# One pool of seven PSUM banks for scores and everything else, with banks and a new order written in the step table

## The reference

```python
qkv = x @ W_qkv                       # 16 heads of 16
q, k = _rope(q, k)
att = einsum('bhtd,bhsd->bhts', q, k) / sqrt(DH) + causal_mask
y = einsum('bhts,bhsd->bhtd', softmax(att), v) @ W_o
x = _layernorm(x + y)
gate = softmax(x @ Wg + bg)           # 8 experts, the 2 largest kept, renormalised
out = einsum('bseo,bse->bso', einsum('bsi,eoi->bseo', x, We) + be, gate_sparse)
x = _layernorm(x + out)
```

## Time and profile before

| | |
|---|---|
| median of 3 runs | 3101.23 us (3095.9 to 3102.56) |
| the profiled execution | 3113.54 us, its span 3111.8 us |
| busy share of the span | PE 95%, DVE 85%, ACT 58%, POOL 34% |
| mean granted clock of TensorE | 0.962 |
| chain that ended last | PE 79%, DVE 13%, issue 4%, DMA 1%, ACT 1% |

### The profile page before, as it was taken

The page is one execution under the profiler, slowest core; times in us unless marked ns, Lnnn a source line. Parts: engine busy times, 40 slices in busy tenths (PEclk is TensorE's granted clock), DMA queues, the critical chain, the costliest instruction groups (busy, mean ns, idle before and its releaser), DMA issues.

```text
span 3111.8 us, 58478 instructions
## 1 busy us (share of the span) xinstructions
PE 2962.5 (95%) x18752; PEld 1400.9 (45%) x18752; DVE 2656.9 (85%) x8449; ACT 1812.8 (58%) x4125; POOL 1053.1 (34%) x1295
## 2 busy tenths in 40 slices
...
DMA packets 136930, 143.84 MB, mean 46 GB/s; under 512 B 29080, under 2 KB 111280, under 8 KB 136368
## 3 DMA queue, kind: packets, MB, share of 16 engines
...
...
## 4 chain that ended last, share of the span: by engine, by line
PE 79%; DVE 13%; issue 4%; DMA 1%; ACT 1%; POOL 0%; SPq 0%; DVEq 0%; ACTq 0%; POOLq 0%
PE bank L1068 26%; PE attend L1164 16%; PE bank L1125 10%; PE scores L1142 9%; PE bank L1105 6%; PE bank L1114 4%; DVE maxima L919 3%; PE bank L1188 3%; DVE bank L916 3%; PE bank L1172 2%; PE bank L1093 1%; DMA x_in<-in_x 1%; PE bank L1179 1%; PE bank L1196 1%; PE bank L1228 1%
## 5 line engine op out<-in xcount | busy, mean ns | idle before, releaser
L787 ACT ACTIVATE weights<-scores 128x512 f32<-128x512 f32 (+3 forms) x3072 | 1330.8, 492 | 836.2 <-PE scores L1142 828.5
L916 DVE CUSTOM_DVE_ANT_0 bank<-bank,far_q 128x128 f32<-128x128 f32 (+3 forms) x2048 | 956.2, 516 | 147.3 <-PE bank L1125 136.2
L919 DVE TENSOR_REDUCE maxima<-bank 128x1 f32<-128x512 f32 x1024 | 646.7, 682 | 50.1 <-PE bank L1125 47.7
L1164 PE MATMUL attend<-weights,values 128*32 128x512 f32 (+3 forms) x6144 | 655.4, 513 | 0.0
L1125 PE MATMUL bank<-k_stack,q_stack 48*128 48x512 f16 (+3 forms) x3072 | 581.2, 340 | 44.3 <-DVE maxima_hi L916 16.8
L706 POOL TENSOR_SCALAR_AFFINE_SELECT weights<-weights 128x512 f32<-128x512 f32 x512 | 320.8, 636 | 883.8 <-ACT weights L787 883.8
L1142 PE MATMUL scores<-q_stack,k_stack 51*128 51x512 f16 (+3 forms) x3072 | 564.2, 337 | 20.9 <-ACT weights L787 10.7
L1125 PEld LDWEIGHTS bank<-k_stack,q_stack 48*128 48x128 f16 x3072 | 174.4, 95 | 478.3 <-issue 315.3
L1142 PEld LDWEIGHTS scores<-q_stack,k_stack 51*128 51x128 f16 x3072 | 169.8, 94 | 448.9 <-ACT weights L787 256.5
L1068 PE MATMUL bank<-wexp_hi,zT_hi 128*128 128x512 f32 x1024 | 366.7, 439 | 2.2
L695 POOL TENSOR_TENSOR rope<-rope,cos_sb 128x512 f32<-128x512 f32 x124 | 158.5, 1278 | 519.3 <-DVE rope_swap L963 519.3
...
## 6 DMA issues: line engine op xcount, KB each, us to landing
parts_scratch<-parts SPq DMA_DIRECT2D x128, 256.0 KB, 2.1
q_stack<-parts_scratch SPq DMA_DIRECT2D x384, 64.0 KB, 2.3
k_stack<-parts_scratch SPq DMA_DIRECT2D x384, 64.0 KB, 2.3
x_in<-in_x SPq DMA_DIRECT2D x64, 256.0 KB, 3.7
...
q_stack<-lowrows SPq DMA_DIRECT2D x384, 4.0 KB, 1.7
...
```

The lines of the kernel that those rows point to most:

```text
L787: act.activation(weights[:, n % NW, hh, c0:CH], st[(QUAD * n + hh) % NS][:, c0:CH], ACT.Exp, scale=DH ** -0.5).then_inc(S["weights_ready"], 1)
L916: dve.tensor_tensor_reduce(out=b[:, 0:w], in0=b[:, 0:w], in1=far_q[:, CH - w:CH], scale=1.0, scalar=-SENTINEL, op0=ALU.add, op1=ALU.max, a ...
L919: dve.tensor_reduce(dst, b[:, 0:w], AX.X, ALU.max).then_inc(fr, 1)
L1164: last = pe.matmul(pv[32 * j:32 * j + 32, c0:CH], values[:, (s + 1) % SLOTS, o:o + 32], weights[:, n % NW, j, c0:CH], start=kb == 0, stop= ...
```

## The change

Three banks for scores and four for the rest become one list `bk` of seven. ST steps get a bank like all others. In `pre`, `early` and `first` the places are as before (score steps in turn over banks 4 to 6, others over 0 to 3). For `mid` and `last` the tables are new: the order of steps differs, and behind each step with a bank stands its bank ("B.1.11.3/3" is step B.1.11.3 in bank 3). `room()` now looks up the last user of the bank in table order, whoever it was: if it was an ST, TensorE waits for that exp, else for the reader's count. The set of steps is the same.

```diff
-NB = 4
+NB = 7
@@ steps(): the word is cut at "/"
+def placed(table):
+    words = (word.partition("/") for word in table.split())
+    return dict(zip(steps(table), (int(b) if b else None for _, _, b in words)))
@@ two rows of the middle table, old and new
-ST.25.0 ST.25.1 B.2.4.0 B.2.4.1 MOE.0.2.3 B.1.8.2 B.1.8.3 YE.1.1 ST.25.2 ST.25.3 PV.24 B.1.9.0 B.1.9.1
-ST.27.0 ST.27.1 MOE.0.3.1 B.1.10.2 B.1.10.3 ST.27.2 ST.27.3 PV.25 PV.26 MASK.27 LOAD.2
+ST.24.0/4 ST.24.1/6 MOE.0.3.1/4 MASK.22 MOE.0.3.2/1 MOE.0.3.3/5 ZT.1.1/0 ZT.1.0/6 YT.1.0/1 ST.24.2/6 ST.24.3/2
+  PV.22 MASK.24 PV.23
+ST.25.0/4 ST.25.1/5 B.1.11.0/0 B.1.11.1/5 B.2.4.0/4 B.2.4.1/2 B.1.11.2/6 B.1.11.3/3 ST.25.2/3 ST.25.3/2 YE.1.1
+  LOAD.2 GL.1/1 QK.1.2/5 GLT.1/0 MASK.25
+ST.27.0/0 ST.27.1/4 B.2.4.2/0 B.2.4.3/5 B.2.5.0/1 B.2.5.1/2 B.2.5.2/3 B.2.5.3/4 ST.27.2/2 ST.27.3/3 PV.26
+  MASK.27
@@ banks()
-        for n, step in enumerate(s for s in plan(seg) if s[0] in BANKED):
-            out[seg, step] = n % NB
+        rest = 0
+        for step in plan(seg):
+            if seg in PLACED and step[0] in ("ST", *BANKED):
+                out[seg, step] = PLACED[seg][step]
+            elif step[0] == "ST":
+                out[seg, step] = NB - NS + (QUAD * step[1] + step[2]) % NS
+            elif step[0] in BANKED:
+                out[seg, step] = rest % (NB - NS)
+                rest += 1
@@ ledger()
+            if step[0] in ("ST", *BANKED):
+                add(f"users{bank(seg, step)}", seg, step)
+def user_before(c, step):
+
+    users = f"users{bank(c.seg, step)}"
+    here = BOOK[users, c.seg]
+    n = here.index(step)
+    while n == 0:
+        if c.seg == "pre":
+            return None, None
+        c = earlier(c)
+        here = BOOK.get((users, c.seg), [])
+        n = len(here)
+    return c, here[n - 1]
@@ TensorE
                 def room():
-                    if c.seg != "pre" or BOOK[f"bank{nb}", "pre"].index(step) > 0:
-                        pe.wait_ge(free[nb], c.below(f"bank{nb}", step, 1))
+                    then, user = user_before(c, step)
+                    if user and user[0] == "ST":
+                        pe.wait_ge(S["weights_ready"], then.at("weights_ready", user))
+                    elif user:
+                        pe.wait_ge(free[nb], then.at(f"bank{nb}", user))
@@ ST
-                    if c.seg not in START or QUAD * n + hh >= NS:
-                        pe.wait_ge(S["weights_ready"], c.below("weights_ready", step, NS))
-                    pe.matmul(st[(QUAD * n + hh) % NS][:, c0:CH], pair(k_stack, MROWS, s, hh, slice(kb * P, (kb + 1) * P)),
+                    room()
+                    pe.matmul(b[:, c0:CH], pair(k_stack, MROWS, s, hh, slice(kb * P, (kb + 1) * P)),
```

More of the change, by code:

```diff
@@ L166 @@
 """)
[L168 to L196, removed]
@@ L203 @@
[L203 to L222, removed]
@@ L232 @@
[L232 to L237, removed]
@@ L277 @@
-ST.47.0 ST.47.1 ST.47.2 ST.47.3 MASK.47 PV.45
-""")
+MIDDLE_TABLE = """
+XL.1
+ST.0.0/4 ST.0.1/0 XL.0 B.0.0.0/2 B.0.0.1/3 PV.46 B.0.0.2/1 B.0.0.3/0 ST.0.2/3 ST.0.3/1 B.0.1.0/4 B.0.1.1/6 MC.3
+  LOAD.0 PV.47 YE.3.1 B.0.1.2/1 B.0.1.3/5 B.0.2.0/2 B.0.2.1/3
+ST.1.0/1 ST.1.1/3 B.0.2.2/4 B.0.2.3/0 XT.0/6 YT.3.1/1 ST.1.2/0 ST.1.3/4 MASK.0 XT.1/5 XL.2 B.0.3.0/3 B.0.3.1/2
+  XL.3
+ST.2.0/4 ST.2.1/3 PV.0 MASK.1 ST.2.2/3 ST.2.3/2 MT.3/6 QK.0.0/1 MASK.2 B.0.3.2/2 B.0.3.3/3
+ST.3.0/0 ST.3.1/1 PV.1 ST.3.2/6 ST.3.3/1 MASK.3 B.0.4.0/6 B.0.4.1/0 ROPE.0.0 B.0.4.2/1 B.0.4.3/2 B.0.5.0/4
+  B.0.5.1/5
@@ new lines @@
+ST.4.0/6 ST.4.1/4 XT.2/3 XR.0 XT.3/6 QK.0.1/0 HT.0.0/6 HT.0.1/1 B.0.5.2/4 B.0.5.3/0 ST.4.2/6 ST.4.3/0 PV.2
+  B.1.0.0/5 B.1.0.1/1 B.1.0.2/4 B.1.0.3/3
+ST.5.0/1 ST.5.1/6 XR.1 ROPE.0.1 B.0.6.0/6 B.0.6.1/2 PV.3 CAST.0.0 YE.0.0 B.1.1.0/1 B.1.1.1/5 ST.5.2/6 ST.5.3/2
+  WO.0.0/0 B.1.1.2/4 B.1.1.3/6
+ST.6.0/0 ST.6.1/3 CAST.0.1 PV.4 ST.6.2/2 ST.6.3/0 B.0.6.2/3 B.0.6.3/1 WO.0.1/2 B.1.2.0/3 B.1.2.1/0
+ST.7.0/0 ST.7.1/2 B.0.7.0/6 B.0.7.1/5 R1.0 HT.1.1/4 QK.0.2/2 B.1.2.2/3 B.1.2.3/4 ST.7.2/6 ST.7.3/1 ROPE.0.2 PV.5
@@ new lines @@
+ST.8.0/5 ST.8.1/2 B.1.3.0/3 B.1.3.1/0 N1A.0 B.1.3.2/6 B.1.3.3/5 PV.6 PV.7 ST.8.2/3 ST.8.3/2 B.1.4.0/4 B.1.4.1/2
+  HT.1.0/1 YT.0.0/6 B.0.7.2/3 B.0.7.3/5 MASK.8
+ST.9.0/3 ST.9.1/4 ZT.0.1/4 B.1.4.2/1 B.1.4.3/2 ST.9.2/3 ST.9.3/5 ZT.0.0/6 QK.0.3/3
+ST.10.0/0 ST.10.1/3 MASK.9 B.0.8.0/5 B.0.8.1/0 CAST.0.2 B.1.5.0/4 B.1.5.1/1 PV.8 ST.10.2/0 ST.10.3/4 MASK.10
+  PV.9
+ST.11.0/5 ST.11.1/2 B.1.5.2/0 B.1.5.3/2 B.0.8.2/5 B.0.8.3/4 B.1.6.0/3 B.1.6.1/1 ST.11.2/6 ST.11.3/0 MASK.11
+  ROPE.0.3 GL.0/6 B.0.9.0/2 B.0.9.1/0
```

167 lines of the change are left out of this document (111 added, 56 removed).

## The result

The changed kernel takes 4857.18 us (median of 4 runs, 4854.05 to 4860.59) against 3100.91 before: ratio 1.5668, 95% interval 1.5641 to 1.5695. It is slower by 57%. The forecast was 4405 in a range of 3950 to 5050.

The account below looks back on a forecast made before the run. TensorE was taken to bound the kernel. Per middle batch 234.7 + 27 + 10 = 272 us, 90 more than 181.9; 14 batches add 1260, the last batch 46, giving 4405 us, range 3950 to 5050.

Parts of the forecast that it names:

- The bound, the shares, what decides: Whole kernel: TensorE bounds it, busy 95% of the span; 14 middle batches of 181.9 us, 82% of the span, decide.
- The new order without banks: Middle batch: TensorE's step prices give 172.3 us against 173.6, 1.3 less per batch; VectorE's and ScalarE's work unchanged.
- The holds: Middle batch: steps waiting for their bank's last user to be read, 92 holds, 62.4 us, giving a batch of 234.7.
- (a): Middle batch: queues on VectorE and ScalarE, plus the old batch's kept waits, add 27 us; bounds 4 and 55.
- (b): Middle batch: TensorE spends a tenth of the batch at the lower clock, adding 10 us; bounds 0 and 50.
- rival "clock": Middle batches: TensorE spends half or more at 1.2 GHz, some 320 us per batch, 5110 us in all; chance 0.22.
- (c): Moved loads, casts and copies of the new order: costed at nothing; 1 to 2 us per batch were LOAD.0's cover gone.
- Floor: Middle batches: only the holds count, queues overlap with them; 238 us per batch, 3940 us in all; chance 0.17.
- Faster: Middle batches: the pool of seven removes 8 us of waits; 174 us per batch, 2993 us in all; chance 0.04.

Follow-up runs that it names:

- filler pair: Changed kernel with bank 6 unused, its steps in the bank counted as released first: 5157.16 us; the same plus idle products fitted into counted holds: 4646.44 us.

## Why the prediction was right or wrong

**The bound, the shares, what decides.** Right. The middle batches carry 1673 of the 1747 us. The last batch added 69 us where I said 46.

**The new order without banks.** Wrong in what it left out. The prices gave 1.3 us less per batch. (The prediction has 90 form changes against 103; counted over the tables, both ways and from one batch into the next, they are 172 against 186. The difference, and so the 1.3 us, is about the same.) In a ring of seven, where bad bank numbers are gone, the new order takes 15 us more per batch than the old one (200.3 against 184.9). The count itself puts 7 of these 15 down to holds (185.1 against 177.9). The step priced TensorE's own time alone and did not ask how the new order sits against banks and VectorE. It mattered little to the result: the holds were counted in the next step with the given banks, and the other 8 are in no term but (a), which was not worked out from them.

**The holds.** Right, and the term that carries the forecast. The count was 234.7 us. In the rows of the changed table that ran wholly at 2.4 GHz (22 of 48 in every middle batch, one more in 13 of the 14) it gives 111.6 us, and 119.9 passed: 7% more. Moving or removing the bank numbers, or halving the ring of four, moved the time in the direction that the count gave, except in the choice among fair places.

**(a) Queues, 27 us.** About right as a sum, though no run shows its parts. What is left of the 67 us beyond the count when (b) is taken off, as measured below, is 24 to 34. The 7% of the full-clock rows would be 16 to 17 us over the batch, so the other rows hold more than their share: row 25, with its five reductions in a row, is one of them. TensorE's idle time in scores held by VectorE, 40.1 us per batch for 27.1 counted, points the same way. A slow matmul lengthens a queue too, so the line between (a) and (b) isn't sharp.

**(b) The clock, 10 us.** This is the step that failed; it was mis-sized by a factor of three to four. I let the mean streaming share, about 65%, stand for the batch and compared it with one stretch of 20 us that kept the full clock at 64%. But the holds are uneven: rows 17 to 22 ran at 2.4 GHz throughout, row 25 at a granted 0.54:

```profile
1067.20:1078.40 11.20, 8.06 (x26) 3.29 (x22) 3.97 (x10) 3.54 (x8) 1.27 (x2) 0.54 0.00 0
```

There TensorE stood 2.61 us and then did GL and QK at half speed, a QK step of 3.1 us (1.9 in the kernel before). A granted mean of 0.83 means that a third of the batch ran at 1.2 GHz, not a tenth. The other 25 rows take 181.5 us where the count gives 123.1, 58 more, clock and queues together. What the clock can have cost of it has an upper bound: by the profile's clock records the 13 batches between the two loads spent 103 us each at 1.2 GHz, and TensorE was busy in 87 of them, by the modelled ends of its matmuls. At 2.4 GHz that work takes half the time, so at most 43 us were lost. The filler pair gives the other side: there such busy time fell from 110 to 22 us per batch, bound 44, and the batch gained 33 to 37. So (b) is 33 to 43 us, an estimate, and 24 to 34 remain for (a). With 27 and 40 the sum would have been 302; that it fits is no further proof, as the two were found by subtraction. By the prediction's own sign, a granted clock under 0.85, the case that came true is the rival "clock", to which I gave 0.22, with half or more of the batch at 1.2 GHz and 320 us. A third of the batch was, and the time lies between that case and the forecast, nearer to the case, and outside the forecast's own range of 4100 to 4660. The wider range held because it reached to that case: that 4857 lies in it is not to the credit of (b). (The last sum is also off by a little: 4420 less 12 is 4408, not 4405.) The section of the Trainium skill that was cited for it ("TensorE: Matmul & The Clock Gate", "A second HAM failure mode: psum-queue depth-cycling") describes this behaviour, and the traces agree: in the six-bank pair 0.79 with holds, 0.97 with holds filled.

**(c) Moves at no cost.** Over the whole span TensorE stood 16.9 us for loads of x and 7.5 us for rows of `q_stack`, against 19.2 and 7.5 us before, so the moves cost nothing that the waits show. They weren't tried one by one, and with holds everywhere their cover grew.

**The rivals.** *Floor* falls: 301 and not 238. *Faster* falls, and the pool's worth in itself was measured: none with the best places counted (1.0009), minus 1.6% in a ring. The stretch of the prelude at 0.70 that spoke for the clock rival was the better witness than the one at 1.00.

## What to carry to other kernels

When banks are named by hand, go through the order once and compare, for each step, the work since the bank's last user began with the time until that user is read; here 92 such places add 62 us to a batch of 182 by the count alone, while all the waits that a better order or placing could have removed were 8. Price a wait of the matrix engine twice: once as the time that it stands, and once as the work behind it at 1.2 GHz where waits come densely, row by row and not by the mean of the batch. A pool shared by users with different readers lets each be held by the others' readers: here it was worth nothing with the best places counted and cost 1.6% in a ring. Whether it pays in a kernel whose waits come from too few banks, no run here tried.

## What the runs showed that I hadn't expected

A kernel got 10% faster by doing work that nobody reads: 174 idle products per batch of 128x128 by 512 columns, placed in waits, brought the granted clock from 0.79 to 0.97 and the time from 5157 to 4646 us. The same kind of filler placed without regard to the length of the wait raised the clock from 0.94 to 0.99 and made its kernel 6.5% slower (4570 to 4866). And a placing that the count calls better (180 against 185 us) was 4% slower (3511 against 3372).
